# Unread TensorE products at five kinds of places in the last stage of a twelve-layer decoder kernel

## The reference, cut to what matters

```python
# L3_attn (retention), H = 16 heads of 8 (keys) and 16 (values)
qk  = jnp.einsum('bhsd,bhtd->bhst', qr, kr) * mask
qk  = qk / jnp.clip(jnp.abs(qk.sum(-1, keepdims=True)), 1.0, None)
out = jnp.einsum('bhst,bhtd->bhsd', qk, vr).transpose(0, 2, 1, 3)
out = (out - out.mean(-1, keepdims=True)) / jnp.sqrt(out.var(-1, keepdims=True) + 1e-05)
out = jax.nn.silu(g) * out.reshape(B, S, H * head_dim)
...
# cross attention, 16 heads of 8, 64 context tokens (layers L2_xattn and L3_xattn)
scores = jnp.einsum('bhqd,bhkd->bhqk', q, k) * scale
out = jnp.einsum('bhqk,bhkd->bhqd', softmax(scores), v)
...
x = _layernorm(x + _L3_attn_ref(x, ...), axis=-1)
x = _layernorm(x + _L3_xattn_ref(x, ctx_1024, ...), axis=-1)
```

## Time and profile before

| | |
|---|---|
| median of 3 runs | 3021.34 us |
| the runs | 3021.34, 3030.97, 3010.86 us |
| the profiled execution: time | 3032.19 us |
| its span, first to last instruction | 3030.4 us |
| PE busy in the span | 2433.6 us (80%) |
| DVE busy | 1693.9 us (56%) |
| granted clock over the span | 0.904 |

### The profile page before, as it was taken

The page is one execution under the profiler, slowest core; times in us unless marked ns, Lnnn a source line. Parts: engine busy times, 40 slices in busy tenths (PEclk is TensorE's granted clock), DMA queues, the critical chain, the costliest instruction groups (busy, mean ns, idle before and its releaser), DMA issues.

```text
span 3030.4 us, 49594 instructions
## 1 busy us (share of the span) xinstructions
PE 2433.6 (80%) x21256; PEld 1655.1 (55%) x21256; DVE 1693.9 (56%) x4103; ACT 1039.5 (34%) x1534; POOL 359.3 (12%) x605
## 2 busy tenths in 40 slices
PE   4665579999999987896688789777897778888788
PEld 2433268777777776664545455444454444455444
DVE  5776736666676655503476533765337752457641
ACT  4454312322233221021233433344333343434442
POOL 0111000011100110173011001110011100111000
PEclk9787679999999999887887999889998899989999
DMA  2000000000000002036400000000000000000000
GB/s 90 1 1 3 1 1 9 2 8 8 9 9 1 9 8 104 12 40 122 129 1 1 1 8 1 1 1 1 8 1 1 1 2 4 4 1 1 1 1 28
DMA packets 39342, 47.93 MB, mean 16 GB/s; under 512 B 7169, under 2 KB 36369, under 8 KB 38354
## 3 DMA queue, kind: packets, MB, share of 16 engines
q1 hardware_dynamic: 33490, 40.43, 4.5%
q0 software_dynamic: 5632, 4.33, 1.1%
HBM read 31.82 MB, written 12.91 MB: 15 GB/s over the span
## 4 chain that ended last, share of the span: by engine, by line
PE 58%; DVE 25%; ACT 8%; issue 4%; POOL 4%; DMA 1%; SPq 0%; DVEq 0%; another core or an unknown queue 0%; ACTq 0%; POOLq 0%
PE banks L2608 7%; DVE wide_area L2481 4%; PE banks L2805 2%; PE banks L1487 2%; PE banks L2355 2%; DVE wide_area L1891 2%; PE banks L1518 2%; PE banks L920 2%; PE banks L1452 2%; PE banks L2364 2%; PE banks L948 2%; PE banks L1799 2%; PE banks L2374 2%; DVE xs L1000 2%; PE banks L2131 1%
## 5 line engine op out<-in xcount | busy, mean ns | idle before, releaser
L2805 PE MATMUL banks<-wA 128*128 128x128 f32 x1394 | 204.7, 293 | 9.8 <-DVE spread L1406 9.8
L2481 DVE TENSOR_REDUCE wide_area<-banks 128x8 f32<-128x2048 f32 x64 | 146.7, 2292 | 106.1 <-PE banks L2355 105.9
L2805 PEld LDWEIGHTS banks<-wA 128*128 128x128 f32 x1394 | 180.7, 203 | 22.3 <-DVE spread L1406 12.0
L2460 ACT ACTIVATE weights<-banks 128x2048 f32<-128x2048 f32 x64 | 120.0, 1877 | 129.7 <-PE banks L2364 129.7
L1007 POOL TENSOR_TENSOR rstd<-moments,eps 128x4 f32<-128x4 f32 x56 | 12.0, 214 | 1170.6 <-DVE moments L996 1170.6
L991 DVE BATCH_NORM_STATS2 stats<-banks 128x6 f32<-128x128 f32 x208 | 50.4, 288 | 169.6 <-PE banks L959 100.6
L1891 DVE TENSOR_REDUCE wide_area<-banks 128x16 f32<-128x1024 f32 x80 | 94.3, 1219 | 47.4 <-PE banks L1784 47.3
L991 DVE BATCH_NORM_STATS2 dilvals<-banks 128x6 f32<-128x128 f32 x144 | 35.2, 288 | 114.4 <-PE banks L959 85.0
L1000 DVE TENSOR_SCALAR xs<-banks,moments,rstd 128x128 f32<-128x128 f32 x208 | 70.7, 402 | 36.1 <-POOL rstd L1009 36.0
L2268 DVE TENSOR_TENSOR weights<-banks,wC 128x1024 f32<-128x1024 f32 x64 | 76.3, 1218 | 22.6 <-PE banks L2131 22.4
L2608 PE MATMUL banks<-wide_area,big 128*128 128x512 f32 x192 | 87.0, 595 | 0.0
(11 more groups left out here) (776 smaller groups left out, 6130.7 us busy)
## 6 DMA issues: line engine op xcount, KB each, us to landing
big<-in_wE SPq DMA_DIRECT2D x1, 4096.0 KB, 12.6
weights<-long_kernel SPq DMA_DIRECT2D x8, 512.0 KB, 7.3
conv<-wide_area SPq DMA_DIRECT2D x16, 256.0 KB, 2.7
wC<-in_wC SPq DMA_DIRECT2D x1, 3012.0 KB, 15.7
wC<-in_wG SPq DMA_DIRECT2D x1, 2971.0 KB, 19.9
big<-in_wT SPq DMA_DIRECT2D x1, 2560.0 KB, 11.1
x_all<-in_xT SPq DMA_DIRECT2D x1, 2048.0 KB, 8.9
total<-spread SPq DMA_DIRECT2D x8, 256.0 KB, 2.3
```

What stands on the lines that cost most here:

```text
L2460: act.activation(m.weights, bank[:, :, :].rearrange("p r c -> p (r c)"), ACT.Exp, scale=DK ** -0.5)\
L2481: return dve.tensor_reduce(m.peaks[:, k % 2, :, :].rearrange("p t (r c) -> p r t c", r=4)[:, :, :, SPARE[j]], m.bank[:, :, :].rearrange("p ...
L2805: pe.matmul(bank[:, 0:P], m.ident, m.ident, start=True, stop=True)
```

## The change

Five entries are added to the table `BUSY`, and nothing else is changed. The strings in `ORDERS` are the same.

```diff
-BUSY = {..., 'far norm': 4, 'gate': 3, 'taken': 20, 'chosen': 5, ...}
+BUSY = {..., 'far norm': 4, 'gate': 3, 'last norm': 1, 'last scores': 1, 'last back': 1, 'retention masked': 1, 'retention turned': 5, 'taken': 20, 'chosen': 5, ...}
```

More of the change, by code:

```diff
@@ L792 @@
 SPARE_PAIR = {0: 16, 1: 17, 2: 0, 3: 1}
-BUSY = {'lead z': 3, 'lead norm': 6, 'lead product': 14, 'out0': 1, 'back0': 5, 'scores1': 1, 'dil_turned0': 2, 'dil_sum0': 2, 'dil_scores1': 1, 'dil_turned1': 4, 'dil_sum1': 2, 'near norm': 12, 'wide start': 1, 'wide out2': 1, 'first3': 6, 'far norm': 4, 'gate': 3, 'taken': 20, 'chosen': 5, 'choice start': 8, 'choice same': 4, 'choice bit': 3, 'choice rank': 40}
+BUSY = {'lead z': 3, 'lead norm': 6, 'lead product': 14, 'out0': 1, 'back0': 5, 'scores1': 1, 'dil_turned0': 2, 'dil_sum0': 2, 'dil_scores1': 1, 'dil_turned1': 4, 'dil_sum1': 2, 'near norm': 12, 'wide start': 1, 'wide out2': 1, 'first3': 6, 'far norm': 4, 'gate': 3, 'last norm': 1, 'last scores': 1, 'last back': 1, 'retention masked': 1, 'retention turned': 5, 'taken': 20, 'chosen': 5, 'choice start': 8, 'choice same': 4, 'choice bit': 3, 'choice rank': 40}
 ORDERS = {
```

## The result

The changed kernel takes 3031.0 us (median of 19 executions, 3022.5 to 3032.7), the kernel before in the same sessions 3013.0 us (median of 19). The ratio is 1.0047, with a 95% interval from 1.0036 to 1.0058: 14 us slower, less than the 1% that was named as the bound. The two medians alone differ by 18 us. Its profiled execution took 3025.8 us, with a span of 3023.9 us.

A forecast was written before the change was run, and what follows sets the result against it. PE was taken as the bound (busy 80%, 58% of the chain, in turns with DVE), partly at a low clock. 33 exposed - 16 - 6 from the clock = +11 us on the 3021.3 us median: 3032 us, range 3002 to 3060.

The forecast's parts named there:

- The gross price: On PE, 192 added products at a mean of 0.258 us each take 49.5 us.
- The hidden part: Waits of PE ahead of the places in the last stage hide 16.5 us of the products; upper bound 21.2 us.
- The exposed cost: Products not hidden come between PE's pieces, behind the other lane's work: 33 us, ends 16 and 49.5 us.
- The clock's return: Last stage's clock rises with PE's share: 16 us back, plus 6 us in the first groups' retention.
- The 6 us for the first groups' retention: Stretch from 1578 to 1609 us at clock 0.50: at most 11.5 us can return, even chance, counted as 6.
- that sign: Last stage's clock in the changed kernel's profile would be 0.92 to 0.93; 0.91 or less, or 0.95 or more, refutes.
- The slopes across stages of different work: Clock against PE's busy share between stretches, 0.69 and 1.2: last stage's clock up 0.010 to 0.017, 12 to 21 us back.
- The place against the waits: A product ahead of its piece's wait fills that wait up to its own length; 67 waits could hide 17.3 us.
- The five ahead of the retention's last transposes: First lane's five delay the other lane's transposes back: 1.1 to 2.1 us on the way to the retention's end.
- that nothing comes back: Last stage's clock stays at 0.91, products cost what they take: 3054 us, or 3071 with nothing hidden; chance 0.15.
- that the clock stays up: Products keep last-stage stretches at the upper level: 61 to 81 us back, 2993 or 2973 us; chance 0.14.

The follow-up runs named there:

- the shorter execution: Profiled execution of the kernel before with only the short stage's 8 products added, its last stage unchanged: 3010.7 us at a clock of 0.916.
- experiment 9: Only the 8 products of the short stage added to the kernel before, last stage unchanged: median 3011.3 us, ratio 0.9991.
- Experiment 11: The changed kernel with all 192 products issued behind the wait of their piece instead of ahead: 3060.2 us, ratio 1.0120 to the kernel before.
- experiment 10: Only 8 products added to the kernel before, in the first groups' retention ahead of the second half of the products with values: 3021.7 us, ratio 1.0009.
- the second profile of before: The kernel before profiled once more without an edit: 3033.6 us.
- experiment 7: The changed kernel with its products using 32 columns of the array instead of 128: 3032.6 us, ratio 1.0049 to the kernel before.
- experiments 2 and 3: Kernel before plus only cross attention's 48 products (3022.4 us, 1.0014), or only the 32 ahead of the retention's second half of products with values (3019.9 us, 1.0007).
- 12: Kernel before plus the 80 products beside narrow ones, cross attention's two places and the retention's masked one: 3025.2 us, ratio 1.0052.

## Why the prediction was right

The sum of +11 us stands against a measured +14 (interval 11 to 17), and the mechanism was the forecast's: a part of the products is hidden in waits, the rest costs, and the clock gives some of it back. That the time, 3031 us, is a microsecond from the forecast's 3032 is luck: the forecast started from the median of three runs, 3021 us, and the kernel before's is 3013 to 3015, so the start was 7 to 8 us too high. The terms were less good than their sum.

*The gross price, 49.5 us.* PE's busy time in the last stage rose by 48.1 us over the shorter execution, for 184 products that were priced at 47.5. But the price of one was wrong in two ways that cancel: at a clock of 0.94 fewer products run at the lower level than was assumed, and beside narrow products one takes 0.32 to 0.42 us at the upper level where 0.22 was taken.

*The hidden part, 16.5 us.* It is larger. The waits right ahead of the places fell by 17 to 19 us, as was read from them, but PE's idle time fell by 25.8 us in all. Of the rest, 2.8 us lie at the scores (L1782 and L1784: 13.1 us of waits in experiment 9, 10.3 in the changed kernel), which the forecast counted as not hidden, and 3.0 at the sums over values (L1808: 21.4 and 18.4), which got no product: one that pushes a piece later also shortens waits further on. Experiment 11 brings 16 us back by taking the cover away.

*The exposed cost, 33 us.* By the busy view it is 48.1 - 25.8 = 22 us, and by the executions at equal clock 26. It was mis-sized by about a fifth because the cover was read too narrowly.

*The clock's return, 22 us.* It is there, but smaller: about 13 us by the executions. The forecast's 30 to 53 us less at the lower level fit the 42 that were found. What they are worth was taken too high, as half of PE's share of them, 0.4 us for each; among the executions of the kernel before 0.01 of the clock, 60 us at the lower level, goes with 17 us, 0.29 for each. The 6 us for the first groups' retention came from a stretch that the shorter execution already runs at the upper level, and experiment 10, with products only there, has no higher clock. The last stage's clock in the profile, 0.94, lies above the 0.92 to 0.93 that were named, but so does experiment 9's without products, so that sign couldn't decide anything. The slopes across stages of different work gave the right size here; no run tests whether they hold as a rule. The two errors, 7 us too much cost and 9 too much return, cancel in the sum. The text saw that the profiled execution lay 10.9 us above the median, and yet took its lower-level time as the kernel's.

*The place against the waits* was right in kind: the order mattered by 22 us (experiment 11), nearly all of it at equal clock (47 against 26). *The five ahead of the retention's last transposes* stand on the chain for 1.12 us, at the low end of the 1.1 to 2.1 us that were given. *The rivals:* that nothing comes back stands against the clocks of 19 executions, and its price of 33 to 49.5 us lies far above the measured 14; that the clock stays up is refuted by the times and by the clock of 0.920, and even twice the products bring it only to 0.925. The forecast text calls the products 2.5% more work; by its own numbers they are 49.5 of 1265.9 us, 3.9%.

By the Trainium skill (TensorE: Matmul & The Clock Gate, Part 1) activity releases the clock and idling lets it fall. The higher clock with the added products (0.920 for 0.913) agrees. The 31 us at 0.50 with PE busy for 29.8 of them stand against it as a full account; the second profile of before has 31 such us too, with PE busy for 29.9; that such a stretch runs at the upper level in other executions of the same instructions (experiment 9), and that the width of the added products made no difference (experiment 7), leaves open what decides it. The Trainium skill says in the same part that the moment of the change varies from run to run. This case agrees that the granted clock does: 0.901 to 0.921 in the 88 executions, and two profiles with the same last stage are 22 us apart.

What stays open: why the returns of the places don't add (experiments 2 and 3 against 12), where in the last stage the return lies, and why both profiles of the kernel before fell on its longer kind of execution. No version faster than the kernel before was found; none of the ten with a ratio has an interval that lies below 1.

## What to carry to other kernels

Before a profile's low clock is counted as something to win, compare the profiled execution's time and clock with those of all executions: here 17 us of the profiled time belonged to that execution and not to the kernel. The same holds afterwards: one profile of each kernel showed no return of the clock, and the clocks of all executions show one. In this stage, with PE busy four fifths of the time, the unread products took 48 us, of which about half lay in waits; the clock gave back about half of what was left, and the kernel was slower all the same. Where they stand matters: ahead of a wait rather than behind it (22 us here), and between pieces of full size one takes 0.22 us, not 0.42.

## What the runs showed of the hardware that was not expected

- A 128x128 product of two records takes 0.22 us between full-size pieces, 0.32 with one neighbour of 32 rows or columns and 0.42 us between two such pieces, all at the upper level; five in a row between transposes 1.12 us.
- The same last stage took 1524.1 us in one execution and 1545.8 us in another, by the clock alone: 0.94 and 0.92, DVE's and ACT's busy time the same to 0.6 us.
- In one profile 31 us went by at 0.50 with PE busy 29.8 us of them, and another execution ran the stretch around it (107 us) at 0.97.
- Over 88 executions of one kernel the granted clock runs from 0.901 to 0.921, and each 0.01 goes with 17 us of 3015. With 192 unread products it is 0.918 to 0.923 in 19 executions; with products of a quarter of the width 0.919 to 0.925 in nine.
